# The wide self-attention's projection, regrouped to 512 tokens with its gathered rows summed on TensorE

## The reference

```
out = yrows.reshape(-1, K, D).sum(axis=1)          # K = 4 gathered expert rows per token, each times its gate
out = out + silu(X @ sw1.T) * (X @ sw3.T) @ sw2.T  # shared expert
x = layernorm(x + out)
# layer 1: N_HEAD = 16, N_KV_HEAD = 4, HEAD_DIM = 64
q, k, v = x @ Wq, x @ Wk, x @ Wv
x1, x2 = q[..., ::2], q[..., 1::2]                 # the same for k
q = concat(x1 * cos - x2 * sin, x1 * sin + x2 * cos)
att = softmax(mask(q k^T / 8)); y = att v; return y @ Wo
```

## Time and profile before

| | us |
|---|---|
| median of 3 runs | 3321.72 |
| the profiled execution's own time | 3317.57 |
| its span, first to last instruction | 3315.8 |
| PE busy | 2489.6 (75%) |
| DVE busy | 1861.2 (56%) |
| ACT busy | 1432.4 (43%) |
| POOL busy | 978.9 (30%) |
| the `l1p` phase, first DMA issue to the first of the next phase | 956.59 to 1181.84 |

### The profile page before, as it was taken

The page is one execution under the profiler, slowest core; times in us unless marked ns, Lnnn a source line. Parts: engine busy times, 40 slices in busy tenths (PEclk is TensorE's granted clock), DMA queues, the critical chain, the costliest instruction groups (busy, mean ns, idle before and its releaser), DMA issues. The chain is left out here.

```text
span 3315.8 us, 43986 instructions
## 1 busy us (share of the span) xinstructions
PE 2489.6 (75%) x15362; PEld 1385.1 (42%) x15362; DVE 1861.2 (56%) x5005; ACT 1432.4 (43%) x2891; POOL 978.9 (30%) x802
## 2 busy tenths in 40 slices
PE   6978886597544668888875669886776788957977
PEld 2323334465332333333353255555443233345666
DVE  4476664465657655555522548324442577655678
ACT  4324442364331146666621414213511355636876
POOL 1045562135455456666621310000201101101200
PEclk9979998798777889999987879998788799968988
DMA  3211100530264421111001210111000322014023
GB/s 110 73 41 41 45 19 30 164 111 27 87 195 79 96 70 34 42 45 40 22 14 51 48 40 1 42 70 33 14 0 26 79 28 35 9 47 121 2 77 102
DMA packets 185740, 182.86 MB, mean 55 GB/s; under 512 B 55161, under 2 KB 152187, under 8 KB 184751
## 3 DMA queue, kind: packets, MB, share of 16 engines
q1 hardware_dynamic: 176110, 167.48, 18.1%
q0 software_dynamic: 9408, 12.56, 2.5%
HBM read 121.81 MB, written 61.59 MB: 55 GB/s over the span
## 5 line engine op out<-in xcount | busy, mean ns | idle before, releaser
L929 POOL TENSOR_TENSOR l1a_p_lo<-res,l1a_p_hi 128x1024 f16<-128x1024 f32 x192 | 311.7, 1642 | 174.1 <-ACT res L1170 174.1
L1179 ACT ACTIVATE l0a_probs<-ps 128x1024 f32<-128x1024 f32 (+1 forms) x192 | 145.6, 810 | 175.2 <-PE ps L1033 103.1
L1179 ACT ACTIVATE l3a_probs<-ps 128x1024 f32<-128x1024 f32 (+1 forms) x192 | 146.6, 808 | 140.5 <-PE ps L1033 113.4
L1169 ACT ACTIVATE l1a_p_hi<-ps 128x1024 f16<-128x1024 f32 x192 | 157.9, 823 | 112.2 <-PE ps L1033 81.6
L1030 PE MATMUL ps<-l1a_qs,l1a_ks 128*128 128x512 f16 (+3 forms) x768 | 165.4, 329 | 32.7 <-ACT res L1170 32.7
L1201 DVE CUSTOM_DVE_ANT_0 l1a_masked<-ps,l1a_wide_mask 128x128 bf16<-128x128 f32 (+3 forms) x256 | 118.0, 489 | 103.0 <-PE ps L999 100.6
L954 POOL TENSOR_TENSOR l0a_both<-l0a_probs 128x768 f32<-128x768 f32 (+2 forms) x96 | 154.5, 1631 | 46.4 <-PE ps L1071 46.1
L999 PE MATMUL ps<-l1a_ks,l1a_qs 128*128 128x512 f16 (+3 forms) x384 | 120.5, 342 | 63.3 <-DVE l1a_nmax L1204 33.1
L2752 PE MATMUL ps<-x_m,x_x 128*128 128x462 f16 (+1 forms) x672 | 135.8, 350 | 31.2 <-PEq L111 30.5
L1170 ACT ACTIVATE res<-ps 128x1024 f32<-128x1024 f32 x192 | 158.5, 826 | 0.0
L1033 PE MATMUL ps<-mask_t,ident_b 128*128 128x128 bf16 x768 | 156.4, 224 | 0.0
(11 more groups left out here) (732 smaller groups left out, 6307.4 us busy)
## 6 DMA issues: line engine op xcount, KB each, us to landing
f_wf<-in_L_ffn_w_dram SPq DMA_DIRECT2D x16, 1024.0 KB
f_slots<-x0a_zeros SPq DMA_DIRECT2D x32, 256.0 KB
f_xe<-f_slots SPq DMA_DIRECT2D x32, 256.0 KB, 3.0
f_ys<-f_y SPq DMA_DIRECT2D x32, 256.0 KB
l1a_qs<-l_q_h SPq DMA_DIRECT2D x64, 128.0 KB
d_wall<-in_L_ffn_W_dram SPq DMA_DIRECT2D x3, 2112.0 KB
l0a_qs<-l_q_h SPq DMA_DIRECT2D x32, 128.0 KB
l0a_ks<-l_k_h SPq DMA_DIRECT2D x16, 256.0 KB
```

What stands on the lines that cost most here:

```text
L929: pool.tensor_tensor(ph_lo[:, n % SLOTS, :, 0:w], probs[:, n % FULL, :, 0:w], ph_hi[:, n % SLOTS, :, 0:w], ALU.subtract).then_inc(s_["low_ ...
L1169: act.activation(ph_hi[:, n % SLOTS, :, 0:w], SB[n % 2][:, :, 0:w], ACT.Exp)
L1179: act.activation(probs[0:KR, n % SLOTS, 2 * pr:2 * pr + 2, 0:w], SB[x % 2][:, :, 0:w], ACT.Exp).then_inc(s_["exps"], 1)
```

## The change

`project_in` loses its rotary part, and `Combine` all but its three buffers. A new function `rotary_projection` (L1819 of the new kernel) does the phase by groups of 512 tokens:

- Four gathered rows are no longer added on VectorE. ScalarE makes a diagonal 128 x 128 matrix of each gate column (`l1p_dg`, L1976), and TensorE sums in PSUM: identity times `d_acc`, to which VectorE has added the residual beforehand (L2064, four operations), plus four diagonal products (L1916, L1921), all in f32. The statistics and the norm read PSUM.
- Weights and normalised tokens are split into f16 high and low parts, once each. A projection is three f16 products for each half of the 256 inputs: high-high, high-low, low-high (L1943 for q and k, L1952 for v).
- A "pair" is now 256 columns by 512 tokens. PSUM slots, `tmp` (which takes over `k.xtr`, in the rows `res`), `st`, `his`, `los` exist twice. A store is 4 DMAs of 128 KB in pieces of 1 KB; before, it was 16 DMAs of 64 KB for 1024 tokens, in pieces of 2 KB.
- 16 gathers stand at the head; those of the next group follow as 6, 5 and 5 before the subtractions of pairs 0, 1, 2 (`GATHERS`). There are 20 slots.
- The next group's statistics stand after pair 3, its norm ahead of pair 4's rotation, its turn after pair 4's projection.

```diff
-def project_in(k, ph, jobs, loads, rope=None, split=False, ahead=None, early=None):
+def project_in(k, ph, jobs, loads, split=False, early=None):
...
-                project_in(k, ph, jobs,
-                           [(w[:, :, 0:FQ], weight_rows(a["L1_attn_Wq"])), (w[:, :, FQ:FQ + FK], weight_rows(a["L1_attn_Wk"])),
-                            (w[:, :, FQ + FK:], weight_rows(a["L1_attn_Wv"])), (cos[:], a["c_cos"]), (sin[:], a["c_sin"])], (cos, sin),
-                           split=True, ahead=combine, early=early)
+                rotary_projection(k, ph, combine, early, qt, kt, v_all, H, KV)
...
-        self.GS = 12
...
+def rotary_projection(k, ph, combine, early, qt, kt, v_all, heads, kv_heads):
...
+    QP = heads // 4
+    PAIRS = QP + kv_heads // 4
+    GS = 20
+    EACH = GT * K0
+    GATHERS = (6, 5, 5, 0, 0)
+    TERMS = [(0, 0), (0, 1), (1, 0)]
...
+    tmp = k.xtr.rearrange("p c n -> p (c n)").rearrange("p (i j n) -> p i j n", i=2, j=4)
+    st = ph.sb("st", [P, 2, 2, GN])
+    parts = [ph.sb(n, [P, 2, 2, GN], F16) for n in ("his", "los")]
+    xp = [ph.sb(f"x{i}", [P, 2, DC, GN], F16) for i in range(2)]
...
+    pairs = [(g, p) for g in range(NG) for p in range(PAIRS)]
...
+            for n, (g, p) in enumerate(pairs):
+                if g == 2 and p == 0:
+                    for i in range(2):
+                        sp.wait_ge(stored[i], 64 * PAIRS)
+                    early.queries(sp)
+                    early.keys(sp)
+                sp.wait_ge(s_["lo_done"], n + 1)
+                sp.sem_inc(s_["storing"], 1)
+                to, r0 = (qt, 4 * DH * p) if p < QP else (kt, 4 * DH * (p - QP))
+                for x, part in zip("hl", parts):
+                    rows = to[x][r0:r0 + 4 * DH, g * GN:(g + 1) * GN].rearrange("(h two r) n -> two h r n", two=2, r=HF)
+                    for half in range(2):
+                        sp.dma_start(rows[half], part[:, n % 2, half, :]).then_inc(stored[n % 2], 16)
...
+            def gather(i0, i1):
+                for i in range(i0, i1):
+                    t, j = divmod(i, K0)
+                    if i >= GS:
+                        pool.wait_ge(s_["combined"], (i - GS) // K0 + 1)
+                    pool.indirect_dma_start(yg[:, i % GS, :], None, combine.ys, bass.IndirectOffsetOnAxis(ap=combine.of_slot[:, t, j:j + 1], axis=0),
+                                            bounds_check=SLOTS0 - 1, oob_is_err=False).then_inc(g_ld[i % GS], 16)
+            gather(0, EACH)
+            for n, (g, p) in enumerate(pairs):
+                if g + 1 < NG:
+                    at = (g + 1) * EACH + sum(GATHERS[:p])
+                    gather(at, at + GATHERS[p])
+                pool.wait_ge(s_["mults"], n + 1)
+                if n >= 2:
+                    pool.wait_ge(s_["lo_done"], n - 1)
+                t = tmp[:, n % 2]
+                pool.tensor_tensor(st[:, n % 2, 0, :], t[:, 0, :], t[:, 2, :], ALU.subtract).then_inc(s_["rotated"], 1)
+                pool.tensor_tensor(st[:, n % 2, 1, :], t[:, 1, :], t[:, 3, :], ALU.add).then_inc(s_["rotated"], 1)
+                if g == 0 and p == PAIRS - 1:
+                    pool.wait_ge(s_["rotated"], 2 * n + 2)
+                    early.fill(pool)
...
+            def summed(t):
+                g = t // GT
+                if t % GT == 0:
+                    pe.wait_ge(s_["summed"], g + 1)
+                    if g:
+                        pe.wait_ge(s_["x_lo"], g)
+                pe.matmul(C[:, t % GT, :], k.ident[:], combine.acc[:, t, :], start=True, stop=False)
+                pe.wait_ge(s_["diag"], (t + 1) * K0)
+                for j in range(K0):
+                    i = t * K0 + j
+                    pe.wait_ge(g_ld[i % GS], 16 * (i // GS + 1))
+                    ins = pe.matmul(C[:, t % GT, :], dg[:, i % EACH, :], yg[:, i % GS, :], start=False, stop=j == K0 - 1)
+                ins.then_inc(s_["combined"], 1)
...
+            def project(n):
+                g, p = pairs[n]
+                if p == 0:
+                    pe.wait_ge(s_["x_lo"], g + 1)
+                if n == 0:
+                    pe.wait_ge(s_["w_lo"], NW)
+                if n >= 2:
+                    pe.wait_ge(s_["mults"], n - 1)
+                for half in range(2):
+                    c0 = (2 * p + half) * P
+                    steps = [(d, m, x) for d in range(DC) for m, x in TERMS]
+                    for i, (d, m, x) in enumerate(steps):
+                        ins = pe.matmul(A[n % 2][:, half, :], wp[m][:, d, c0:c0 + P], xp[x][:, g % 2, d, :], start=i == 0, stop=i == len(steps) - 1)
+                    ins.then_inc(s_["jobs_done"], 1)
...
+            for t in range(GT):
+                summed(t)
+            columns(0)
+            for n, (g, p) in enumerate(pairs):
+                project(n)
+                if p == 0:
+                    rows(g)
+                if g + 1 < NG:
+                    for t in {1: (0,), 2: (1, 2), 3: (3,)}.get(p, ()):
+                        summed((g + 1) * GT + t)
+                    if p == PAIRS - 1:
+                        columns(g + 1)
...
+            def diagonals(i0, i1):
+                for i in range(i0, i1):
+                    t, j = divmod(i, K0)
+                    if i >= EACH:
+                        act.wait_ge(s_["combined"], t - GT + 1)
+                    act.activation(dg[:, i % EACH, :], k.ident[:], ACT.Copy, scale=combine.weight[:, j, t:t + 1]).then_inc(s_["diag"], 1)
...
+            def upper(n):
+                act.wait_ge(s_["rotated"], 2 * n + 2)
+                if n >= 2:
+                    act.wait_ge(stored[n % 2], 64 * (n // 2))
+                act.activation(parts[0][:, n % 2, :, :], st[:, n % 2, :, :], ACT.Copy).then_inc(s_["hi_done"], 1)
+            diagonals(0, EACH)
+            act.wait_ge(s_["w_ld"], 48)
+            for i in range(NW):
+                act.activation(w_flat[1][:, i * 1024:(i + 1) * 1024], w_flat[0][:, i * 1024:(i + 1) * 1024], ACT.Copy).then_inc(s_["w_hi"], 1)
+            roots(0)
+            columns(0)
+            for n, (g, p) in enumerate(pairs):
+                if g + 1 < NG and p < 2:
+                    diagonals((g + 1) * EACH + 2 * p * K0, (g + 1) * EACH + 2 * (p + 1) * K0)
+                if p == 1:
+                    rows(g)
+                if p < PAIRS - 1:
+                    upper(n)
+                if p == PAIRS - 2 and g + 1 < NG:
+                    roots(g + 1)
+                if p == PAIRS - 1:
+                    upper(n)
+                if p == PAIRS - 1 and g + 1 < NG:
+                    columns(g + 1)
...
+            def moments(g, half):
+                dve.wait_ge(s_["combined"], g * GT + 2 * half + 2)
+                for j in range(2 * half, 2 * half + 2):
+                    ch.step(dve.bn_stats(stats[:, g * GT + j, :], C[:, j, :]))
...
+            def normal(g):
+                dve.wait_ge(s_["sd_ready"], g + 1)
+                dve.reciprocal(rs[:, g, :], sd[:, g, :]).then_inc(s_["rs_ready"], 1)
+                dve.wait_ge(s_["rs_ready"], g + 1)
+                for j in range(GT):
+                    t = g * GT + j
+                    ins = dve.tensor_scalar(k.xr[:, t, :], C[:, j, :], mv[:, t, 0:1], rs[:, g, j:j + 1], ALU.subtract, ALU.mult)
+                ins.then_inc(s_["xn_ready"], 1)
...
+            def rotate(n):
+                g, p = pairs[n]
+                at = slice(g % 2 * GN, (g % 2 + 1) * GN)
+                if n == 0:
+                    dve.wait_ge(s_["t_ld"], 32)
+                if n >= 2:
+                    dve.wait_ge(s_["rotated"], 2 * (n - 2) + 2)
+                for half, (f, o) in enumerate(((cos, sin), (sin, cos))):
+                    dve.wait_ge(s_["jobs_done"], 2 * n + half + 1)
+                    dve.tensor_tensor(tmp[:, n % 2, 2 * half, :], A[n % 2][:, half, :], f[:, at], ALU.mult)
+                    ins = dve.tensor_tensor(tmp[:, n % 2, 2 * half + 1, :], A[n % 2][:, half, :], o[:, at], ALU.mult)
+                ins.then_inc(s_["mults"], 1)
...
+            for g in range(NG):
+                rows = slice(g * GT, (g + 1) * GT)
+                dve.tensor_tensor(combine.acc[:, rows, :], combine.acc[:, rows, :], k.xr[:, rows, :], ALU.add).then_inc(s_["summed"], 1)
+            for i in range(NW):
+                dve.wait_ge(s_["w_hi"], i + 1)
+                at = slice(i * 1024, (i + 1) * 1024)
+                dve.tensor_tensor(w_flat[2][:, at], w_flat[0][:, at], w_flat[1][:, at], ALU.subtract).then_inc(s_["w_lo"], 1)
+            moments(0, 0)
+            moments(0, 1)
+            variances(0)
+            normal(0)
+            columns(0)
+            for n, (g, p) in enumerate(pairs):
+                last = p == PAIRS - 1
+                if last and g + 1 < NG:
+                    normal(g + 1)
+                rotate(n)
+                if n and p:
+                    lower(n - 1)
+                if g + 1 < NG and p == PAIRS - 2:
+                    moments(g + 1, 0)
```

(6 more changed lines are left out.)

254 lines of the change are left out of this document (83 added, 171 removed).

## The result

The changed kernel took 3328.80 us (median of 20 runs, 3322.49 to 3337.88), the kernel before 3320.27 beside it (20 runs): 1.0026 times as long, 95% interval 1.0016 to 1.0037, 8.5 us slower. Forecast were 3294 and 27.4 less. No median or ratio in this document contains an execution in the chip's second, slower state.

The account below looks back on a forecast made before the run. No engine was full, so order was taken to decide, with about 34 us idle at the start. Start, three laps of 43.1, last group and a shorter end gave 27.4 us less: 3290.2, with 4.15 added 3294; range 3271 to 3314.

Parts of the forecast that it names:

- phase start to first subtraction: Start of the projection: first product at 990, then a pair 5.1 and 1.3, so first subtraction at 996.4.
- three laps: Three groups of 512 tokens, each a chain of 43.1 us through GpSimd and its crossings, ending at 1125.7.
- last group to its low part's end: Last group: five pairs at 4.4, so 22, and 2.2 for high and low part; last low part at 1149.9.
- from there to the next phase: End of the projection: 4 store issues, 1.8 us, and 2.7 from the last issue; next phase at 1154.4.
- All at 175 it is 27 of 43 us: DMAs of one lap: all gathers and stores at 175 GB/s take 27 us of the lap's 43.
- Rival 4: Projection laps: stores in 1 KB pieces, or gathers behind them, set the lap, 50 us; whole kernel 3320; chance 0.07.
- The attention's instructions don't change: Attention behind the projection: its instructions stay the same, and no time was added for it.
- rival 1: Projection: TensorE stays at 1.2 GHz and becomes the bound, lap 57, whole kernel 3345; chance 0.09.
- rival 3: Projection: the chain isn't serial, laps are GpSimd's own 34.1, whole kernel 3267; chance 0.08.
- The exclusion: Projection laps: VectorE's low part and GpSimd's operations on SBUF shut each other out; 1.15 charged twice per lap.
- rival 2: Turns between groups: TensorE waits some 8 us, its clock drops, 3 us a lap, whole kernel 3303; chance 0.08.
- a mean of 0.8: Lap: clock taken as 0.8 for TensorE's 5.7 us on the chain, making the 41.6 us lap 43.1.

Follow-up runs that it names:

- a_pairs: Changed kernel with the fill ahead of the first rotation and queries and keys stored in blocks of four heads and 512 tokens: 3311.3 us, ratio 0.9975.
- a_fill_cut: Changed kernel ended behind the projection, with GpSimd's memsets moved ahead of the first rotation: 1190.9 us, against 1193.2 without the move.
- b_late: Kernel before, with the attention's loads of queries and keys issued behind the next step's column sums, maxima and inverse rows: 3290.2 us, ratio 0.9913.
- a_pairs_late: Changed kernel with early fill, blocks of four heads and 512 tokens, and the attention's loads one step later: 3295.4 us, ratio 0.9888 to the kernel before.

## Why the prediction was wrong

By its own steps, in us:

| step | predicted | after | `a_pairs` |
|---|---|---|---|
| phase start to first subtraction | 39.8 | 41.1 | 42.1 |
| three laps | 129.3 | 142.1 (47.9, 43.8, 50.4) | 136.5 (45.1, 45.3, 46.1) |
| last group to its low part's end | 24.2 | 27.7 | 23.2 |
| from there to the next phase | 4.5 | 10.5 | 4.3 |
| projection | 197.8 | 221.3 | 206.0 |
| attention, against 472.7 | 0 | +8.3 | +8.1 |

1. **The stores' rate is the step that failed in the sum.** "All at 175 it is 27 of 43 us" took a rate from stores that reach sixteen engines for stores that reach four. By `a_pairs` it is worth 15 of the 23.5 us by which the projection missed: last group 4.5, end 6.2 and 5.6 in the laps, less the memsets' 1.5. Rival 4 had the place and nearly the size (laps of 50, 3320) with the wrong cause, pieces of 1 KB, and was priced at 0.07 against a share of at most 0.52: the share speaks for engines that a DMA reaches, not for the DMA.
2. **"The attention's instructions don't change" was taken for "its time doesn't".** This step cost 8.3, twice the 4.0 that the projection gained in the same profile. No trace of before was read there; its waits of 2.4 to 3.5 for `l1a_y_col`, in every other step, would have shown 23 us to be had.
3. **The memsets** that the diff puts between pair 4 and the gathers were in no lap: 3.6 in the first, of which 1.5 were uncovered (`a_fill_cut`).
4. **The order was read rightly.** 25 us came off the start (the first product stands 35.6 behind the phase's start, 60.3 before, 33.4 predicted), the mean clock is 0.76 to 0.86 and TensorE has idle pieces (rival 1 fell), and GpSimd has gaps (rival 3 fell). The exclusion was charged rightly too: in each of the three laps of `a_pairs`, two of five pairs take GpSimd 3.4 or 3.5 instead of 2.5.
5. **The clock at the turns: rival 2 came true.** The laps' own chain is 45.1 to 46.1 with good stores, 2 to 3 more than 43.1. The sum spread a mean of 0.8 over the 5.7 us of TensorE's work that lie on the chain, 1.5 in all. But this work stands directly behind TensorE's waits, where the clock is low. At the three turns of `a_pairs`, behind 7.3 to 8.0 of waiting, pair 0's products take 5.1, 4.2 and 5.3 instead of 2.75, and pair 3's, behind the waits for gathers, 3.7, 5.3 and 4.6. Together that is 3.3 to 4.4 a lap against the 1.5, which is the 2 to 3. Rival 2 priced it at 3 a lap for the turn alone, with a chance of 0.08. No run holds the clock up there, so this is read from the traces and not tested.

So two terms of the projection were mis-sized, the stores' rate and the clock at the turns, and one term outside it was put at nothing.

Then why was before so near? Its projection had 34 us at the start and slack behind, as predicted, but its stores reached sixteen engines. The change gave that up for half the issues.

What stays open: with the attention's difference taken away by the late loads, the changed kernel is still 9.7 slower than the kernel before on the same chip (0.9948 against 0.9913), while the attentions are equal and the projections differ by 4.5 in the two profiles. So the 8.3 of the attention are measured, with and without the stages behind them, but that they and nothing else make the 8.5 of the whole kernel is not shown. The rest of the kernel, behind the attention, took 1660 us in the profile of before and 1669 to 1679 in all other whole kernels, the longest in `b_late`, whose profiled execution was the slowest of its six. By the phases `a_pairs_late` should gain 15 on `b_late` in the projection; by the ratios it gains 8. And why SyncE's stretched issues sit where they do was not found.

## What to carry to other kernels

Write a DMA so that its outermost dimension, on both sides, is 16 or a multiple, and count the packets beside the data to see how many engines it reached: here a share of 0.2 with an even rate was a quarter of the engines. Where an unchanged stage follows a change, look in its trace for waits, above all for a small urgent DMA behind a batch of loads on one queue; put the urgent one first. Where work on a chain stands directly behind a wait of TensorE, price it by a row at the low clock level, not by the mean clock of the stretch. An explanation that fits one experiment (fewer pieces) needs a second one that holds the rest fixed.
